# A graph network's attention layer on one core: the first tile of each attention step searched from GpSimd's guess alone

## The reference

```
for s in range(2):
    logits = (Xa @ W1) @ W2 @ (Xa @ W3).T
    # per row: sort downwards, keep the entries until the softmax mass reaches 0.9
    A = softmax(where(kept, logits, -inf))
    Xf = Rf @ Xf;  Xb = Rb @ Xb;  Xa = A @ Xa       # Rf, Rb: adj + I, normalised by row and column sums
    Z = Z + (Xf @ U1[s] + Xb @ U2[s] + Xa @ U3[s])
Y = layernorm(X + Z) * gamma + beta
```

## Time and profile before

| | us |
|---|---|
| median of 3 runs | 3476.09 (3475.62 to 3479.3) |
| the profiled execution | 3477.54 |
| its span, first to last instruction | 3475.8 |
| TensorE, VectorE, GpSimd, ScalarE busy | 3141.6, 2449.9, 2154.7, 1598.2 |
| attention: first row maximum to last L1444 | 807.5 to about 3212 |

### The profile page before, as it was taken

How to read it: one execution, slowest core, us unless ns; L and a number is a source line. 1 busy time by engine, 2 the same in 40 slices (tenths; PEclk the granted TensorE clock), 3 DMA queues, 4 the chain that set the end, 5 groups by cost and what they waited for, 6 DMA issues and landing times. The chain is left out here.

```text
span 3475.8 us, 42043 instructions
## 1 busy us (share of the span) xinstructions
PE 3141.6 (90%) x13212; PEld 2270.6 (65%) x13212; DVE 2449.9 (70%) x3401; ACT 1598.2 (46%) x2357; POOL 2154.7 (62%) x4214
## 2 busy tenths in 40 slices
PE   4999989997799999999976689988899999996899
PEld 3888778885567777777754255544566666664788
DVE  6840123333998889888883799999988999998000
ACT  2311322225666666666653445545555555652100
POOL 2212421114788888888881677878988788886211
PEclk9999999998899999999988899999999999998899
DMA  7644344433112222122111111211222222233255
GB/s 254 241 146 145 116 151 167 165 130 87 44 54 59 61 63 60 57 60 64 57 37 58 47 56 53 57 48 51 58 82 75 78 80 82 74 87 99 96 197 173
DMA packets 140702, 327.59 MB, mean 94 GB/s; under 512 B 15456, under 2 KB 93664, under 8 KB 129248
## 3 DMA queue, kind: packets, MB, share of 16 engines
q1 hardware_dynamic: 140512, 325.30, 29.5%
HBM read 286.70 MB, written 38.54 MB: 94 GB/s over the span
## 5 line engine op out<-in xcount | busy, mean ns | idle before, releaser
L1025 ACT ACTIVATE junk<-E,negp 128x3327 uint8<-128x3327 f32 x208 | 637.3, 3064 | 141.3 <-issue 107.3
L1397 DVE SCALAR_TENSOR_TENSOR U<-E,trial 128x3327 f32<-128x3327 f32 x182 | 678.1, 3726 | 0.0
L920 PE MATMUL bank<-big,adj 128*128 128x512 f32 x1352 | 608.7, 601 | 8.7 <-ACT t L1051 8.7
L920 PEld LDWEIGHTS bank<-big,adj 128*128 128x128 f32 x1352 | 252.4, 192 | 328.9 <-issue 327.9
L297 PE MATMUL bank<-big,E 128*128 128x256 f32 x1664 | 366.7, 382 | 2.8 <-PEq L58 1.7
L880 PE MATMUL bank<-Hc,PT 128*128 128x256 f32 x1248 | 303.1, 395 | 65.5 <-ACT PT L1064 65.4
L880 PE MATMUL bank<-Hc,adj 128*128 128x256 f32 x1456 | 338.0, 384 | 16.4 <-ACT adj L1064 16.2
L297 PEld LDWEIGHTS bank<-big,E 128*128 128x128 f32 x1664 | 315.8, 191 | 50.3 <-issue 5.7
L1359 DVE TENSOR_REDUCE nmax<-E 128x1 f32<-128x3327 f32 x52 | 188.0, 3615 | 208.8 <-ACT E L1068 208.8
L880 PEld LDWEIGHTS bank<-Hc,adj 128*128 128x128 f32 x1456 | 279.5, 193 | 79.8 <-issue 22.5
L880 PEld LDWEIGHTS bank<-Hc,PT 128*128 128x128 f32 x1248 | 244.3, 198 | 126.3 <-ACT PT L1064 77.0
(11 more groups left out here) (248 smaller groups left out, 5750.2 us busy)
## 6 DMA issues: line engine op xcount, KB each, us to landing
adj<-adjT SPq DMA_DIRECT2D x131, 448.0 KB, 3.4
E<-adjT SPq DMA_DIRECT2D x32, 1664.0 KB, 6.9
adj<-adjT SPq DMA_DIRECT2D x104, 384.0 KB, 3.3
adj<-adjT SPq DMA_DIRECT2D x20, 1664.0 KB, 7.0
E<-adjT SPq DMA_DIRECT2D x26, 1216.0 KB, 5.8
xt<-xin SPq DMA_DIRECT2D x52, 128.0 KB, 5.8
x_d<-xn SPq DMA_DIRECT2D x52, 128.0 KB, 1.7
xt<-x_d SPq DMA_DIRECT2D x52, 128.0 KB, 5.3
```

The source lines that it names most:

```text
L920: last = mm(agg[:, 0:w], adj[:, SPAN * (k % 2) + j - AGG[k]], rhs[:, j], start=(j == 0), stop=False)
L1025: go(junk[:, 0:N], E[:, t % DEPTH, 0:N], func, bias=negp[:, t % 2, j:j + 1], scale=1.0, accum_out=acc_[:, t % 2, j:j + 1]).then_inc(summed ...
L1397: V_.scalar_tensor_tensor(out=U[:, 0:N], in0=e, scalar=point, in1=e, op0=ALU.is_ge, op1=ALU.mult, accum_out=found))
```

## The change

Tiles 0 and 26 (`unaided`) lose ScalarE's four sums passes, both `update`s, the offers and the `prepare`. Their guess is made without the shift of the mean (`SHIFT` is 1.4 in step 1, 0 in step 2), copied into the search's first point, and `bracketed` is raised at the end of `guess`. `find` makes 4 evaluations for tile 0 and 5 for tile 26, and it is issued in round 2 (round 33), right behind the row maximum of tile 1 (tile 27), and so ahead of the row maximum of tile 2 (tile 28); before, it came behind that one. ScalarE gets one new wait: its first score copy of tile 2 (tile 28) waits for `bracketed` of tile 0 (tile 26). The other edits renumber the semaphores (`aided`).

```diff
+ALONE = (4, 5)
+            unaided = lambda t: t % NT == 0
+            aided = lambda t: t - 1 - t // (NT + 1)
...
                                 if L is not None:
                                     w, c0 = WIDE[k] * P, BLK[k] * P
                                     act.wait_ge(lg_done, SLOTS * L + k + 1)
+                                    if k == 0 and L >= 2 and unaided(L - 2):
+                                        act.wait_ge(bracketed, L - 1)
...
-                                if k == 0 and R is not None:
+                                if k == 0 and R is not None and not unaided(R):
                                     sums(R, 1, 0)
...
-                                if k == 3 and F is not None:
+                                if k == 3 and F is not None and not unaided(F):
                                     sums(F, 0, 1)
...
-                                 ts(ga_(8), ga_(5), 1.0, -SHIFT[step], ALU.mult, ALU.add))
+                                 ts(ga_(8), ga_(5), 1.0, 0.0 if unaided(t) else -SHIFT[step], ALU.mult, ALU.add))
...
-                            offer(t, 0)
+                            if not unaided(t):
+                                offer(t, 0)
...
-                            prepare(t)
+                            if unaided(t):
+                                then(ts(trial2[:, d, POINT:POINT + 1], p, 1.0, None, ALU.mult))
+                                pool.sem_inc(bracketed, 1)
+                            else:
+                                prepare(t)
...
-                            if R is not None:
+                            if R is not None and not unaided(R):
                                 update(R, 1)
...
-                            if F is not None:
+                            if F is not None and not unaided(F):
                                 update(F, 0)
...
-                            for k in range(EVALS[step]):
+                            for k in range(ALONE[step] if unaided(t) else EVALS[step]):
...
                             if F is not None:
                                 row_max(F)
-                            if S is not None:
+                                if unaided(F - 1):
+                                    find(F - 1)
+                            if S is not None and not unaided(S):
                                 find(S)
```

More of the change, by code:

```diff
@@ L1015, in sums @@
                         def sums(t, j, m):
+                            a = aided(t)
                             if m == 0:
-                                act.wait_ge(aimed[j], t + 1)
+                                act.wait_ge(aimed[j], a + 1)
                                 if j > 0:
-                                    act.wait_ge(summed[j - 1], PASSES[j - 1] * (t + 1))
-                                elif t >= 1:
-                                    act.wait_ge(summed[1], 2 * t)
+                                    act.wait_ge(summed[j - 1], PASSES[j - 1] * (a + 1))
+                                elif a >= 1:
+                                    act.wait_ge(summed[1], 2 * a)
                             else:
-                                act.wait_ge(summed[j], 2 * t + 1)
+                                act.wait_ge(summed[j], 2 * a + 1)
                             func, acc_ = ((ACT.Relu, over), (ACT.Sign, sign))[m]
@@ L1245, in update @@
                             count, mass_ = up_(5 + j), up_(8 + j)
-                            pool.wait_ge(summed[j], PASSES[j] * (t + 1))
+                            pool.wait_ge(summed[j], PASSES[j] * (aided(t) + 1))
                             then(ts(count, sign[:, q, j:j + 1], 0.5, N / 2, ALU.mult, ALU.add))
```

## The result

The changed kernel takes 3481.52 us (median of 20 runs, 3479.53 to 3484.28), the kernel before, beside it, 3476.19: the ratio is 1.0017, with a 95% interval of 1.0010 to 1.0024, so 3.5 to 8.3 us slower. The profiled execution took 3481.56 us with a span of 3479.8, 4.0 over the one before. All runs shown here were in the same, fast state, but for one of the ten executions of the first run with fewer evaluations: it took 11368.78 us, for which nothing shows a reason, and the ratio of that run leaves it out.

A forecast was written before the change was run, and what follows sets the result against it. TensorE was taken to set the pace mid-step 1 and later in step 2, VectorE at step 2's start; only the two starts could matter. Median 3476.09 plus 5.5 (+6.4 step 1, -0.9 step 2) gave 3481.6 us, range 3463 to 3495.

The forecast's parts named there:

- no change within 0.2%: Whole kernel: the time stays within 0.2%, 7 us, of the kernel before; chance 0.44, against slower 0.39 and faster 0.17.
- The mechanism: Step 1: tile 2's row maximum, queued behind tile 0's earlier search, delays ScalarE's exponential and tile 3's score copies; +6.4 us.
- the rounds: Searches of tiles 0 and 26: extraction rounds assumed 2 and 3, as before; 8.9 us each; chance 0.28.
- Start and length of the searches: VectorE, step 1: tile 0's search starts at 830.6, 21.1 us earlier, and ends at 876.2 with one more evaluation, 5.32 us.
- The chain behind row maximum 2: Step 1: exponential of tile 2 at 879.8, copies to 898.3, row maximum 3 6.4 us later, TensorE's round 4 8.2 later.
- Step 2: Start at tile 26: search from 1904.9 to 1965.6, row maximum 29 at 1987.0 instead of 1987.86, -0.9 us.
- the estimate for the restart at TensorE's lower clock: TensorE at the start of step 2: twelve wide matmuls' instructions take 1.6 us more than 5.42.
- The port: VectorE and GpSimd sharing: tile 1's offer slips to near 850.8, hidden under VectorE's search; taken as 0 us.
- the 3.3 us kept for the range: VectorE's six long search passes may lose at worst 3.3 us to GpSimd in each step; taken as 0, kept as margin.
- rival of more rounds: VectorE's search of tile 0 or 26 needs one or more extra extraction rounds, 8.9 us each: 3490.5 and more; chance 0.31.
- Rival 3: Both starts: tile 2's row maximum holds nobody; TensorE takes tile 0 15.8 us and tile 26 22.3 us earlier, 3438; chance 0.04.

The follow-up runs named there:

- the first run with fewer evaluations: The changed kernel with 3 and 4 evaluations instead of 4 and 5 for tiles 0 and 26: 3480.15 us, ratio 1.0011 to the kernel before.

## Why the prediction was right, and where it wasn't

The forecast was 3481.6, the median is 3481.52; no change within 0.2% was called the likeliest, and 0.17% slower is that, though the interval reaches 0.24% and leaves out zero. The mechanism was right in step 1, where the loss is. That the sum is met to 0.1 us is luck: 5.5 was forecast, the two starts of the trace give 4.1, and the interval of the times is 3.5 to 8.3. It is luck too that the rounds came out as taken, which the forecast itself gave 0.28. Step by step, from row maximum 0 and 26:

- **Start and length of the searches.** Predicted 23.1 behind row maximum 0 and 45.6 long; measured 829.88 - 806.77 = 23.1 and 45.5. In step 2 predicted 16.7 and 60.7; measured 16.6 and 59.8.
- **The chain behind row maximum 2.** Predicted row maximum 3 at 898.3, 6.4 later; measured 6.7 later. The exponential was put at 879.8 - 807.47 = 72.3 and stood at 72.3; TensorE's round 4 was put 8.2 later and came 899.67 - 806.77 - 84.62 = 8.3 later. That this chain is the cause is shown by moving the row maximum.
- **Step 2.** Predicted 0.9 earlier, measured 2.6. The term mis-sized is the time to row maximum 29: the search was 0.9 shorter (see the last section), and behind it exponential, copies and TensorE's twelve instructions took 20.7 where 21.4 was worked out. Most of that is the estimate for the restart at TensorE's lower clock: the twelve took 6.48 us (1984.70 above), 1.1 over the 5.42 of before and not 1.6. The granted clock was 0.50 in 1978:1985 and 0.81 in 1985:1990.
- **The port.** The slowed GpSimd was there, but the offer of tile 1 came at 845.43 + 0.22 and not near 850.8: more of the guess fitted between VectorE's passes than was worked out. It was costed at nothing, and ScalarE's wait of 25.02 behind it shows that it is. L1408 had no longer passes in the moved searches (mean 3676 ns in step 1's, 3678 in step 2's), so the 3.3 us kept for the range found no place. By the rule of the Trainium skill (SBUF — State Buffer, "SBUF: two separate sides") each of them might have waited for a GpSimd operation; these passes show no such wait. On VectorE's short instructions see the last section.
- **The rounds.** 2 and 3 were taken for want of a row, and are what the trace has. That was an assumption that held, not a step that was understood: it rests on the dropped shift for tile 0 (3 rounds with it) and on the fifth evaluation for tile 26 (4 rounds without it), and the prediction gave the shift no price at all. Had either been otherwise, its rival of more rounds would have been the outcome: 3490.5 in its terms, for one round more.
- **Rival 3**, that the row maximum of tile 2 holds nobody, is wrong for the change as written, and most of what it described is what one moved instruction gives: 12.5 and 19.4 us of its 15.8 and 22.3 (3447 and 3444; the rival had 3438). What is missing in each start is near the 3.6 us of the row maximum, which now stands in the search.

## What to carry to other kernels

When a long step is moved forward in an engine's program, list what it is moved past: here one 3.6 us reduction went behind a 45 us search, another engine's in-order queue hung on it, and 16 us of earlier end became 7 us of loss. Here the long step had a place in its middle for the short one, and that was worth 32 us; look for such a place before giving a move up. And where a loop's trip count depends on data, measure the count by itself with one evaluation more and one fewer, as each may be worth less than its cost on one tile and more on another.

## What was not expected of the hardware

Some of VectorE's short instructions took between twice and four and a half times as long as usual, each time beside one of GpSimd's instructions on 128x256. In tile 26's search before, these rows stand side by side in the timelines of VectorE and GpSimd; the first is the same VectorE instruction two evaluations earlier:

```profile
1936.87 0.16 DVE L1388 TENSOR_TENSOR sc<-ends 128x1 f32<-128x1 f32 x1
...
1947.46 0.72 DVE L1388 TENSOR_TENSOR sc<-ends 128x1 f32<-128x1 f32 x1
...
1948.37 0.50 DVE L1391 SCALAR_TENSOR_TENSOR sc<-ends,sc 128x1 f32<-128x1 f32 x1
...
1949.34 0.36 DVE L1396 TENSOR_SCALAR ends<-ends 128x2 f32<-128x2 f32 x1
```

```profile
1947.43 0.73 POOL L1294 TENSOR_TENSOR t<-t 128x256 f32<-128x256 f32 x1
1948.12 0.73 POOL L1295 TENSOR_TENSOR xt<-xt 128x256 f32<-128x256 f32 x1
1948.93 0.74 POOL L1301 TENSOR_TENSOR adj<-t,xt 128x256 f32<-128x256 f32 x1
```

Usually the three take 0.16, 0.20 and 0.16 us, so this makes 1.1 us, and the search of tile 26 came out 0.9 shorter than predicted in the changed kernel. There GpSimd's three, at 1946.72 to 1948.94, fell beside the first extraction round, and none of the three was longer than usual. With the searches at the old place they fell into the evaluations again, and the same three VectorE instructions took 0.72, 0.50 and 0.35 us. In the whole trace of the kernel before, 54 of the 442 instructions of these three lines took over 0.3 us, and every one of the 54 overlaps a GpSimd instruction on 128x256; none is long beside GpSimd's operations on one number per row, of which its updates are made. 18 others overlap one too and kept their usual time, so the overlap alone isn't enough. That the port is the reason was not tried by itself.
